# Four buffers for the down weights of a mixture of experts, and the last two items brought to their tokens by TensorE

## The chip, the core and the metric

The kernel runs on one core of a Trainium2 chip. The time is the device time of one execution in microseconds (us); less is better. The core has TensorE (PE, matmuls), VectorE (DVE), ScalarE (ACT), GpSimd (POOL) and SyncE (SP), each with an instruction stream of its own, and 16 DMA engines that all of them share. The engines meet at semaphores only.

## What is computed

A block of three layers on 512 tokens (8 sequences of 64) of width 512: cross attention, a linear attention, and a mixture of experts. The change is in the third alone:

```python
logits = xf @ gate_w.T                        # 512 tokens, 32 experts
top_w, top_i = lax.top_k(softmax(logits), 6)
h  = silu(einsum('ecd,edi->eci', xb, w1)) * einsum('ecd,edi->eci', xb, w3)   # xb: the tokens of each expert
ob = einsum('eci,eid->ecd', h, w2)            # w1, w3: 512 x 352, w2: 352 x 512 for each expert
y  = zeros((T, D)).at[t_s].add(ob[buf_idx] * w_s[:, None])
return x + y + silu(xf @ sw1) * (xf @ sw3) @ sw2
```

All of it is in float32.

## The kernel before

The first two layers take the first 690 us and are not touched. In the third, the shared experts are done as 8 items (`NSH`: two halves of the weights by four tiles of 128 tokens), while the router's result is turned into lists. Then come the **items** of the routed experts. An item is one expert with up to 128 of its tokens; an expert that has more than 128 gets a second item, next in the list. Here there are 36 items for 32 experts, so four items (1, 6, 13 and 26, counted from 0) are the second of their expert. How many there are, and which, is known only on the chip, so each engine runs a loop of two items a turn up to a value read from the list (`last_turn`), and reads what it needs for item m from rows of a small list in SBUF, `lst`, into a register: `item_value`, one read for one value. `ODD` of m is 1 if item m - 1 is a second item, `LOADED` is 1 if the item's weights are to be loaded, `HIGH` is half of m, `SLOT` says which of the two split copies of the up weights its expert has.

For item m the engines do this:

- **GpSimd** gathers 128 token rows three items ahead (`ex_gather`, indirect DMA) and scatters the result of item m - 2 with an addition into one of two arrays in HBM, `y_scratch` (`ex_scatter`, indirect DMA).
- **SyncE** issues the loads: `ex_load_w13` (two DMAs of 704 KB, for w1 and w3, into one of four raw slots of `w13_raw`), and `ex_load_w2` (512 KB and 192 KB, into one of **two** slots of `w2_raw`). A load whose expert is already there is issued with a condition that is 0, and moves nothing. In a turn the queue handles the up weights of item m + 3, then the down weights of item m. The latter wait until the down matmuls of item m - 2 are done (`d_ps`).
- **ScalarE** and **VectorE** split the raw up weights into a high and a low part (L888 and L892), as float32 is multiplied in three passes (`mm3`, L311 to L313).
- **TensorE** transposes the next item's tokens, does 24 up matmuls of item m (`ex_up`), the down matmuls of item m - 1 (`ex_down`, L876; these wait for the down weights, `w2_in`), and transposes h (`ex_hT`).

The queue's waits for down weights before:

```python
            if isinstance(m, int) and m == 0:
                e.wait_ge(d_ps, TT)
            else:
                e.wait_ge(d_ps, m + item_value(e, ODD, m) + (NSH - 1))
```

After the last item its result and the one before are scattered too. Then SyncE reads both `y_scratch` arrays back (L1176, L1179), VectorE adds them to x (L1661, L1665), and SyncE writes x out (L1182).

Of the kernel before, what the change touches and what calls it, by code (L numbers as in the profile page):

```python
# [31 lines left out]
P = 128  # L32
# [6 lines left out]
def perceiver_block(nc, x_in, ctx_in, ctxT_in, Wq, Wk, WkT, Wv, Wo, gq, gk,  # L39
# [17 lines left out]
    with stack:  # L57
# [144 lines left out]
        hot = sbuf(moe, "hot", [P, TT, TOP_K, E])  # L202
        hotp = sbuf(moe, "hotp", [P, TT, TOP_K, E])
# [7 lines left out]
        seats_and_items = sbuf(moe, "seats_and_items", [P, TT * TOP_K * (P + 2 * ML)])  # L211
        seat = seats_and_items[:, 0:TT * TOP_K * P].rearrange("p (q n) -> p q n", n=P)
        item = seats_and_items[:, TT * TOP_K * P:].rearrange("p (q a n) -> p q a n", a=2, n=ML)
        y_back = seats_and_items[:, 0:2 * TT * D].rearrange("p (k t d) -> p k t d", k=2, t=TT)
# [16 lines left out]
        EXPERT, LOADED, SLOT, ODD, HIGH = range(5)  # L231
        lst_f = sbuf(moe, "lst_f", [1, 5, ML + 1])
        lst_j = sbuf(moe, "lst_j", [1, ML + 1])
        lst = sbuf(moe, "lst", [1, 5, ML + 1], I32)
# [3 lines left out]
        w2_raw = sbuf(moe, "w2_raw", [P, 2, FC, D])  # L238
# [57 lines left out]
        y0_in, y1_in = sem("y0_in"), [sem(f"y1_in{t}") for t in range(TT)]  # L296
        y_sum, out_ready = sem("y_sum"), sem("out_ready")
# [581 lines left out]
        def raw_slot(e, m, k):  # L879

            if isinstance(m, int):
                return m % 4
            return item_value(e, HIGH, m) * 2 + k
# [40 lines left out]
        def ex_pe(e, i, k, first=False):  # L924

            m = i * 2 + k
            e.wait_ge(xeT_ready, m + 1)
            ex_pe_xT(e, 1 - k, i + (k + 1))
            e.wait_ge(h_ready, m + (NSH - 1))
            ex_up(lambda c: xeT_h[:, k, c, :], lambda c: xeT_l[:, k, c, :], k, item_value(e, SLOT, m), m * 2 + 6)  # L930
            ex_down(e, 1 - k, m + (NSH - 1), 1 if first else item_value(e, SLOT, m - 1),
                    (w2_in[1], 32) if first else (w2_in[1 - k], i * 32 + (k + 1) * 32), m + (NSH - 2))
            ex_hT(e, k, m + NSH)

        def ex_act(e, i, k):

            m = i * 2 + k
            odd = item_value(e, ODD, m + 1)
            ex_act_hT(e, 1 - k, m + (NSH - 1))
# [5 lines left out]
            raw = raw_slot(e, m + 1, 1 - k)  # L945
# [3 lines left out]
        def ex_dve_ob(e, i, k):  # L949

            m = i * 2 + k
            if not isinstance(i, int) or i > 1:
                e.wait_ge(acc_done[k], i * 16 - 16)
            e.tensor_copy(give[:, k:k + 1], tl[:, bass.ds(m - 2, 1)]).then_inc(give_ready, 1)
            e.wait_ge(d_ps, m + (NSH - 1))
            e.tensor_scalar(ob[:, k, :], ps[:, 6 + k, :], wl[:, bass.ds(m - 2, 1)], None, ALU.mult).then_inc(d_read, 1)  # L956
# [8 lines left out]
        def ex_dve(e, i, k):  # L965

            m = i * 2 + k
            ex_dve_xT(e, m + 1, 1 - k)
            ex_dve_take(e, m + 3, 1 - k)
            if isinstance(i, int) and i == 0:  # L970
                ex_dve_x(e, NSH - 2 + k)
            else:
                ex_dve_ob(e, i, k)
            ex_dve_h(e, k, m + NSH)
            if not isinstance(m, int) or m > 0:
                raw = raw_slot(e, m + 1, 1 - k)
# [15 lines left out]
        def ex_pool_scatter(e, m, k):  # L992

            e.wait_ge(give_ready, m - 1)
            e.wait_ge(d_read, m + (NSH - 1))
            e.sem_inc(acc_turn, 1)
            ex_scatter(e, k)

        def ex_pool(e, i, k):
# [6 lines left out]
            if not isinstance(i, int) or i > 0:  # L1006
                ex_pool_scatter(e, m, k)
# [4 lines left out]
        def load_w2(e, k, whole_ap, rest_ap, **cond):  # L1012
            e.dma_start(w2_raw[:, k, 0:FC - 1, :], whole_ap, **cond).then_inc(w2_in[k], 16)  # L1013
            e.dma_start(w2_raw[0:FW[-1], k, FC - 1, :], rest_ap, **cond).then_inc(w2_in[k], 16)  # L1014
# [8 lines left out]
        def ex_load_w13(e, m, k, before):  # L1023

            ex, new, raw = item_value(e, EXPERT, m, E - 1), item_value(e, LOADED, m), raw_slot(e, m, k)
            for n, w in enumerate((w1_r, w3_r)):
                if not isinstance(m, int) or m >= 2:
                    e.wait_ge(w13_ready, m * 2 + (n - 3))
                e.wait_ge(w13_in[k][n], before * 16)
                cond = {} if isinstance(m, int) and m < 2 else {"cond": new}  # L1030
                load_w13(e, k, n, raw, w[bass.ds(ex, 1)].rearrange("e p c f -> p (e c) f"), **cond)

        def ex_load_w2(e, m, k):
            ex, new = item_value(e, EXPERT, m, E - 1), item_value(e, LOADED, m)
            if isinstance(m, int) and m == 0:
                e.wait_ge(d_ps, TT)
            else:
                e.wait_ge(d_ps, m + item_value(e, ODD, m) + (NSH - 1))
            load_w2(e, k, w2_r[bass.ds(ex, 1)].rearrange("e p c d -> p (e c) d"),
                    w2_t[bass.ds(ex, 1)].rearrange("e p d -> p (e d)"), cond=new)  # L1040

        def last_turn(e):

            e.wait_ge(small_dve, DV_LISTS)
            return e.value_load(lst[0:1, EXPERT, ML:ML + 1], min_val=T * TOP_K // P // 2 - 1, max_val=MI // 2 - 1)

# [8 lines left out]
        def _(e):  # L1055
# [96 lines left out]
            def shared_rest():  # L1152
                for k in range(2):
                    load_w2(e, k, w2_r[E + k], w2_t[E + k])
# [9 lines left out]
            ex_load_w2(e, 0, 0)  # L1164
# [11 lines left out]
            e.dma_start(y_back[:, 0, :, :], y_dram[0].ap()[0:T, :].rearrange("(t p) d -> p t d", p=P)).then_inc(y0_in, 16)  # L1176
            e.wait_ge(acc_done[1], last_i * 16 + 16)
            for t in range(TT):
                e.dma_start(y_back[:, 1, t, :], y_dram[1].ap()[t * P:(t + 1) * P, :]).then_inc(y1_in[t], 16)  # L1179
# [3 lines left out]
            for k in range(2):  # L1183
                for s, n, uses in ((w13_in[k][0], 16, 5 - k), (w13_in[k][1], 16, 5 - k), (w2_in[k], 32, 3)):
                    e.wait_ge(s, last_i * n + uses * n)
                    e.sem_inc(past_loads, 1)
            e.wait_ge(past_loads, 6)
# [3 lines left out]
        def _(e):  # L1191
# [50 lines left out]
            e.tensor_tensor(gw_l[:, :, :], gw_raw[:, :, :], gw_h[:, :, :], ALU.subtract).then_inc(small_lo, 1)  # L1242
            last_i = last_turn(e)
# [9 lines left out]
            with e.Fori(2, last_i + 1) as i:  # L1253
                ex_pool(e, i, 0)
                ex_pool(e, i, 1)
            for k in range(2):
                ex_pool_scatter(e, last_i * 2 + (k + 2), k)

        @block.scalar
        def _(e):  # L1260
# [115 lines left out]
            ex_act_w13(e, 1, 0, 2, 1)  # L1376
            ex_act_w13(e, 1, 1, 2, 1)
# [3 lines left out]
            with e.Fori(1, last_act + 1) as i:  # L1381
                ex_act(e, i, 0)
                ex_act(e, i, 1)
            ex_act_hT(e, 1, last_act * 2 + (NSH + 1))

        @block.vector
        def _(e):
# [191 lines left out]
            def lists():  # L1579
# [9 lines left out]
                step(e.tensor_copy(lst_f[0:1, HIGH, 0:ML], iota_e[0:1, 0:ML]))  # L1589
                step(e.tensor_copy(lst[0:1, :, :], lst_f[0:1, :, :]))  # L1590
                step(e.tensor_scalar(lst[0:1, HIGH, 0:ML], lst[0:1, HIGH, 0:ML], 1, None, ALU.arith_shift_right))
                step(e.tensor_scalar(lst[0:1, EXPERT, ML:ML + 1], lst[0:1, EXPERT, ML:ML + 1], 1, None, ALU.arith_shift_right))
                e.tensor_scalar(lst[0:1, SLOT:HIGH + 1, :], lst[0:1, SLOT:HIGH + 1, :], 1, None, ALU.bitwise_and).then_inc(small_dve, 1)
# [54 lines left out]
            ex_dve_w13(e, 1, 0, 7, 1)  # L1648
            ex_dve_xT(e, 0, 0)
            ex_dve_take(e, 2, 0)  # L1650
            ex_dve_w13(e, 1, 1, 8, 1)
            for m in range(4):
                ex_dve(e, m // 2, m % 2)
            with e.Fori(2, last_i + 1) as i:
                ex_dve(e, i, 0)
                ex_dve(e, i, 1)
# [201 lines left out]
```

## Time and profile before

| | |
|---|---|
| median of 3 runs | 1063.48 us (1063.03 to 1066.78) |
| profiled execution: its own time | 1069.81 us |
| its span | 1068.0 us |
| granted TensorE clock, mean | 0.982 |
| PE busy in the span | 986.1 us (92%) |
| DVE, ACT, POOL busy | 62%, 51%, 25% |

The profile shows one execution. Its span begins with the first instruction; times in the rows are microseconds from there. Its own time is 6.3 us above the median of the runs without a profile, so differences are to be taken between profiled executions, or between medians. An engine's busy time doesn't count instructions that only handle registers, semaphores or the issue of DMAs; SyncE has no other kind, so the table has no row for it. `SPq` in a view is SyncE's stream.

### The profile page before, as it was taken

What the parts mean: (1) busy time and instruction counts of PE and PEld (TensorE: products, weight loads), DVE (VectorE), ACT (ScalarE), POOL (GpSimd) and SP (SyncE); (2) the same over time, 40 slices, a digit from 0 to 9 for tenths busy, and PEclk for the clock granted to TensorE, in tenths of its full rate; (3) what the DMA queues carried; (4) which work ended last, traced back from release to release, by engine and by line L of the source; (5) the groups of instructions that cost most, each with busy time, mean ns of one, the idle gap of its engine ahead of it and who ended that gap; (6) DMA issues with size and microseconds to landing.
All of it is one profiled execution on the core that took longest, in us unless ns stands there. A gap on an engine that the chain in (4) does not pass through costs nothing.

```text
span 1068.0 us, 18826 instructions
## 1 busy us (share of the span) xinstructions
PE 986.1 (92%) x5428; PEld 824.3 (77%) x5429; DVE 666.2 (62%) x994; ACT 543.1 (51%) x888; POOL 272.0 (25%) x188
## 2 busy tenths in 40 slices
PE   6999899999999869999999998799998999998792
PEld 5788699898998748888888886588776776776681
DVE  5645665667656557777777875557466666666563
ACT  5444666665666545555555525332454554554451
POOL 2200122121221133333222414200132232232222
PEclk9899999999999999999999999899999999999997
DMA  9000452332125041222112024106489999999986
GB/s 314 31 0 1 107 183 81 98 98 76 45 76 130 1 148 60 79 66 70 59 60 98 20 104 159 59 1 255 147 255 276 297 276 352 336 292 279 316 238 184
DMA packets 76059, 152.92 MB, mean 143 GB/s; under 512 B 11264, under 2 KB 38272, under 8 KB 75776
## 3 DMA queue, kind: packets, MB, share of 16 engines
q1 hardware_dynamic: 67728, 132.92, 37.1%
q0 software_dynamic: 8304, 19.67, 8.6%
q8 instruction: 14, 0.23, 0.1%
q14 instruction: 13, 0.11, 0.0%
HBM read 153.87 MB, written 14.55 MB: 158 GB/s over the span
## 4 chain that ended last, share of the span: by engine, by line
PE 63%; issue 12%; SPq 11%; DVE 4%; DMA 4%; ACT 3%; POOL 2%; ACTq 0%; DVEq 0%; POOLq 0%
PE ps L311 15%; PE ps L312 15%; PE ps L313 15%; SPq L847 6%; PE ps L672 6%; PE ps L876 4%; DMA w_raw<-in_w 2%; SPq L1010 2%; POOL wo_l L451 1%; SPq L1013 1%; SPq L1014 1%; PE ps L731 1%; PE ps L738 1%; PE ps L748 1%; PE ps L659 1%
## 5 line engine op out<-in xcount | busy, mean ns | idle before, releaser
L876 PE MATMUL ps<-w_raw,hT 128*128 (+3 forms) x264 | 124.3, 607 | 20.2 <-DMA w_raw<-in_w 17.8
L892 DVE TENSOR_TENSOR w_l<-w_raw,w_h 128x1408 fp32r<-128x1408 f32 x78 | 124.8, 1639 | 21.9 <-issue 13.2
L888 ACT ACTIVATE w_h<-w_raw 128x1408 fp32r (+1 forms) x78 | 103.3, 1369 | 25.1 <-issue 16.0
L694 POOL TENSOR_TENSOR lw_l<-lw_raw,lw_h 128x1024 fp32r<-128x1024 f32 x32 | 77.0, 2409 | 146.6 <-ACT lw_h L690 146.1
L985 POOL DMA_INDIRECT xe<-xn_scratch,take x39 | 39.2, 1004 | 259.1 <-DVE ob L956 173.2
L876 PEld LDWEIGHTS ps<-w_raw,hT 128*128 128x128 f32 (+1 forms) x264 | 48.0, 191 | 68.0 <-issue 67.7
L311 PE MATMUL ps<-w_h,xeT_h 128*128 x288 | 96.6, 335 | 1.6 <-DVE w_l L892 1.6
L313 PE MATMUL ps<-w_h,xeT_l 128*128 x288 | 93.4, 324 | 0.0
L312 PE MATMUL ps<-w_l,xeT_h 128*128 x288 | 92.9, 323 | 0.0
L311 PE MATMUL ps<-xT_hi,lw_h 128*128 128x512 f32 x192 | 77.3, 402 | 0.0
L312 PE MATMUL ps<-xT_lo,lw_h 128*128 128x512 f32 x192 | 76.5, 398 | 0.0
L901 DVE TENSOR_TENSOR h<-h,ps 128x352 f32<-128x352 f32 x44 | 22.9, 521 | 85.7 <-PE ps L313 59.8
L313 PE MATMUL ps<-xT_hi,lw_l 128*128 128x512 f32 x192 | 75.4, 393 | 0.0
L1395 DVE TENSOR_REDUCE ssk<-sqk 128x4 f32<-128x512 f32 (+1 forms) x64 | 43.6, 685 | 39.4 <-ACT sqk L1275 39.2
L906 ACT ACTIVATE hT<-ps 128x256 f32<-128x256 f32 x44 | 16.8, 383 | 99.5 <-PE ps L865 99.3
L1275 ACT ACTIVATE sqk<-ps 128x512 f32<-128x512 f32 x64 | 38.1, 598 | 49.8 <-PE ps L313 43.9
L311 PE MATMUL ps<-wk_h,cT_h 128*128 128x512 f32 (+1 forms) x128 | 52.2, 408 | 11.3 <-DVE cT_l L1391 8.7
L554 POOL TENSOR_TENSOR wq_l<-wq_raw,wq_h 128x1024 fp32r<-128x1024 f32 x8 | 19.3, 2411 | 170.0 <-ACT wq_h L514 170.0
L672 PE MATMUL ps<-pT,ctx 128*128 128x128 f32 x512 | 61.9, 277 | 0.4
L989 POOL DMA_INDIRECT y_scratch<-ob,give x36 | 57.2, 1588 | 15.8 <-issue 10.4
L672 PEld LDWEIGHTS ps<-pT,ctx 128*128 128x128 f32 x512 | 59.0, 192 | 2.0 <-ACT pT L544 2.0
L785 DVE RECIPROCAL q_r<-q_r 128x512 f32<-128x512 f32 x16 | 53.6, 3348 | 6.0 <-ACT q_r L761 6.0
(297 smaller groups left out, 2610.4 us busy)
## 6 DMA issues: line engine op xcount, KB each, us to landing
w_raw<-in_w SPq DMA_DIRECT2D x86, 704.0 KB
w_raw<-in_w SPq DMA_DIRECT2D x40, 512.0 KB
w_raw<-in_w SPq DMA_DIRECT2D x40, 192.0 KB
rkB<-rk_scratch SPq DMA_DIRECT2D x56, 128.0 KB, 3.2
wq_raw<-in_Wq SPq DMA_DIRECT2D x8, 512.0 KB, 4.7
wo_raw<-in_Wo SPq DMA_DIRECT2D x16, 256.0 KB, 2.9
lw_raw<-in_kwT SPq DMA_DIRECT2D x8, 512.0 KB, 3.4
lw_raw<-in_qwT SPq DMA_DIRECT2D x8, 512.0 KB, 3.3
```

The lines of the kernel that those rows point to most:

```text
L311: nc.tensor.matmul(out_ap, lh, rh, start=first, stop=False)
L312: nc.tensor.matmul(out_ap, lh, rl, start=False, stop=False)
L313: return nc.tensor.matmul(out_ap, ll, rh, start=False, stop=last)
L672: m = e.matmul(ps[:, 4 + j % 2, at:at + P], ctx[:, b * KPB + t, hcol(c)], pT[:, b, t, :], start=t == 0, stop=t == KPB - 1)
L694: e.tensor_tensor(lw_l[n][:, :, :], lw_raw[n][:, :, :], lw_h[n][:, :, :], ALU.subtract).then_inc(lw_ready[n], 1)
L785: e.reciprocal(q_r[:, k, :], q_r[:, k, :]).then_inc(q_recip, 1)
L847: return e.value_load(lst[0:1, row, bass.ds(m, 1)], min_val=0, max_val=most)
L876: m = e.matmul(ps[:, 6 + k, :], hT[r, k, c, :], w2_raw[r, slot(w), c, :], start=c == 0, stop=c == FC - 1)
L888: e.activation(w13_h[:, k, n, :, :], w13_raw[:, slot(raw), n, :, :], ACT.Copy).then_inc(w13_hi_s, 1)
L892: e.tensor_tensor(w13_l[:, k, n, :, :], w13_raw[:, slot(raw), n, :, :], w13_h[:, k, n, :, :], ALU.subtract).then_inc(w13_ready, 1)
L989: e.indirect_dma_start(y_dram[k].ap(), bass.IndirectOffsetOnAxis(ap=give[:, k:k + 1], axis=0), ob[:, k, :], None, compute_op=ALU.add).then ...
L1395: e.tensor_reduce(ssk[:, t, bass.ds(g * 4, 4)], sqk[:, t % 2, :].rearrange("p (h n) -> p h n", n=P), AX.X, ALU.add).then_inc(sqk_free, 1)
```

## The change

It does five things.

1. **Four down-weight slots.** `w2_raw` has four slots. They lie partly over the seats and items lists, which are dead once the tokens are listed, and the loads of items 2 and 3 wait for that (`small_ps`). An item's down weights are asked for four items ahead in SyncE's order and wait for the down matmuls of item m - 4.
2. **The expert's first slot.** `HIGH` gives way to `FIRST`, the raw slot of the expert's first item (0 to 3); a second item takes up and down weights from there. A slot is then in use an item longer, so a new row `HELD` says by how many items the wait is later. `LOADED` now holds for item 1 as well.
3. **The last turn is peeled** from the loops of all engines: no token transposes, gathers and splits for items behind the last. SyncE's loop ends two turns earlier, and GpSimd's and VectorE's one, with the turn ahead read from the list.
4. **The last two items go to tokens by TensorE**: VectorE makes `home` (128 seats by 512 tokens, 1 where the seat's token is the column), and TensorE multiplies it with the items' results into four banks of PSUM, which VectorE adds to x. They are not scattered.
5. **Order at the end**: SyncE waits for all loads before it reads y back, since y now lies over other tiles.

```diff
         def ex_load_w13(e, m, k, before):
 
-            ex, new, raw = item_value(e, EXPERT, m, E - 1), item_value(e, LOADED, m), raw_slot(e, m, k)
+            ex, new = item_value(e, EXPERT, m, E - 1), item_value(e, LOADED, m)
+            static = isinstance(m, int) and m < 4
+            raw, held = (m, 0) if static else (raw_slot(e, m), item_value(e, HELD, m, 3))
             for n, w in enumerate((w1_r, w3_r)):
-                if not isinstance(m, int) or m >= 2:
+                if not static:
+                    e.wait_ge(w13_ready, m * 2 + (held * 2 + (n - 3)))
+                    e.sem_inc(acc_turn, 1)
+                elif m >= 2:
                     e.wait_ge(w13_ready, m * 2 + (n - 3))
...
-        def ex_load_w2(e, m, k):
+        def ex_load_w2(e, m, k, before):
+
             ex, new = item_value(e, EXPERT, m, E - 1), item_value(e, LOADED, m)
-            if isinstance(m, int) and m == 0:
-                e.wait_ge(d_ps, TT)
+            w = m if isinstance(m, int) and m < 4 else raw_slot(e, m)
+            if isinstance(m, int) and m < 2:
+                e.wait_ge(d_ps, TT * (m + 1))
+            elif isinstance(m, int) and m < 4:
+                e.wait_ge(small_ps, PS_TOKENS)
             else:
-                e.wait_ge(d_ps, m + item_value(e, ODD, m) + (NSH - 1))
-            load_w2(e, k, w2_r[bass.ds(ex, 1)].rearrange("e p c d -> p (e c) d"),
+                e.wait_ge(d_ps, m + item_value(e, HELD, m, 3) + (NSH - 3))
+                e.sem_inc(acc_turn, 1)
+            e.wait_ge(w2_in[k], before * 32)
+            load_w2(e, k, w, w2_r[bass.ds(ex, 1)].rearrange("e p c d -> p (e c) d"),
                     w2_t[bass.ds(ex, 1)].rearrange("e p d -> p (e d)"), cond=new)
...
             for m in (2, 3, 4):
                 ex_load_w13(e, m, m % 2, m // 2 + 1)
-            ex_load_w2(e, 1, 1)
+            for m in (1, 2, 3):
+                ex_load_w2(e, m, m % 2, m // 2 + 1)
             for m in range(2):
                 ex_load_w13(e, m + 5, 1 - m, m + 3)
-                ex_load_w2(e, m + 2, m)
-            with e.Fori(1, last_i + 1) as i:
+                ex_load_w2(e, m + 4, m, 3)
+            with e.Fori(1, last_i - 1) as i:
                 for k in range(2):
                     ex_load_w13(e, i * 2 + (k + 5), 1 - k, i + (k + 3))
-                    ex_load_w2(e, i * 2 + (k + 2), k)
-            e.wait_ge(acc_done[0], last_i * 16 + 16)
...
+                    ex_load_w2(e, i * 2 + (k + 4), k, i + 3)
...
+            e.wait_ge(past_loads, 6)
+            e.wait_ge(acc_done[0], last_i * 16)
+            e.dma_start(y_back[0][:, :, :], y_dram[0].ap()[0:T, :].rearrange("(t p) d -> p t d", p=P)).then_inc(y0_in, 16)
...
+            for k in range(2):
+                e.tensor_scalar(home[:, k, :], iota_t[:, :], tl_f[:, 1, bass.ds(last_i * 2 + k, 1)], None,
+                                ALU.is_equal).then_inc(home_ready, 1)
...
+            e.wait_ge(home_ready, 2)
+            e.wait_ge(d_read, last_i * 2 + (NSH + 1))
+            to_tokens(0, 0)
+            ex_down(e, 1, last_i * 2 + (NSH + 1), item_value(e, FIRST, last_i * 2 + 1, 3), (w2_in[1], last_i * 32 + 64),
                     last_i * 2 + NSH)
+            for t in range(1, TT):
+                to_tokens(0, t)
+            e.wait_ge(d_read, last_i * 2 + (NSH + 2))
+            for t in range(TT):
+                to_tokens(1, t).then_inc(last_ps, 1)
```

What the built program has on **SyncE** in its loop, for the down weights of one item, before (`TENSOR_LOAD lst` reads one value of the list, `ISA` and `REGISTER_ALU` are instructions on registers):

```order
L847 ISA
L847 TENSOR_LOAD lst
L847 ISA x3
L847 TENSOR_LOAD lst
L847 ISA x3
L847 TENSOR_LOAD lst
L847 ISA x2
L1038 ISA
L1013 ISA [waits d_ps]
L1013 DMA w_raw<-in_w 128x1024
L1014 ISA
L1014 DMA w_raw<-in_w 96x512
```

The same place in the changed program, up to the wait for the DMA two items earlier:

```order
L852 ISA
L852 TENSOR_LOAD lst
L852 ISA x3
L852 TENSOR_LOAD lst
L852 ISA x3
L852 TENSOR_LOAD lst
L852 ISA x3
L852 TENSOR_LOAD lst
L852 ISA x2
L1058 ISA
L1060 REGISTER_ALU [waits d_ps]
L1025 ISA [waits w2_in0]
```

and on from there:

```order
L1025 REGISTER_ALU
L1025 DMA w_and_lists<-in_w 128x1024
L1026 ISA
L1026 REGISTER_ALU
L1026 DMA w_and_lists<-in_w 96x512
```

There are four reads for three, and three short instructions more. The up weights have a read more as well. Over the loop's two items the changed stream has 16 reads, 60 `ISA` and 7 `REGISTER_ALU`; the one before has 12, 52 and 2.

At the end of **TensorE**'s stream, before (the down matmuls of the last item):

```order
L870 REGISTER_ALU
L872 REGISTER_ALU [waits hT_ready]
L873 ISA [waits d_read]
L876 ISA [waits w2_in1]
L876 MATMUL ps<-w_raw,hT 128x512
L876 ISA
L876 MATMUL ps<-w_raw,hT 128x512
L876 ISA
L876 MATMUL ps<-w_raw,hT 128x512
L57 UNCONDITIONAL_BRANCH
```

and in the changed program:

```order
L1862 MATMUL ps<-ob,hots 128x512 [waits d_read,home_ready]
L852 ISA
L852 TENSOR_LOAD lst
L852 ISA x2
L881 ISA [waits w2_in1,d_read,hT_ready]
L881 MATMUL ps<-w_and_lists,hT 128x512
L881 ISA
L881 MATMUL ps<-w_and_lists,hT 128x512
L881 ISA
L881 MATMUL ps<-w_and_lists,hT 128x512
L1862 MATMUL ps<-ob,hots 128x512 x3
L1862 MATMUL ps<-ob,hots 128x512 [waits d_read]
```

One token matmul stands ahead of the last down matmuls, three behind them, and four more (the last row and three like it) wait for the last item's scaled result.

## Rows read from the trace of the kernel before

**Rows 1.** The page, part 2: busy tenths in 40 slices, the DMA engines.

```profile
DMA  9000452332125041222112024106489999999986
```

**Rows 2.** The waits, 760 to 1068: us in total, times, longest.

```profile
PE ps L876 <- DMA w_raw<-in_w: 17.8, 12, 2.4
```

**Rows 3.** The waits of SyncE's queue, 760 to 1060.

```profile
SPq L1013 <- PE ps L876: 38.9, 5, 16.2
```

**Rows 4.** TensorE's timeline, first up matmuls of three items: start, duration.

```profile
756.10 0.42 PE L311 MATMUL ps<-w_h,xeT_h 128*128 x1
...
1031.40 0.40 PE L311 MATMUL ps<-w_h,xeT_h 128*128 x1
...
1038.68 0.40 PE L311 MATMUL ps<-w_h,xeT_h 128*128 x1
...
1042.48 0.33 PE L313 MATMUL ps<-w_h,xeT_l 128*128 x1
```

**Rows 5.** SyncE's timeline, 765 to 1048: issues of up (L1010) and down weights (L1013).

```profile
777.82 0.34 SPq L1013 DMA_DIRECT2D w_raw<-in_w  x1
...
786.72 1.05 SPq L1010 DMA_DIRECT2D w_raw<-in_w  x2
...
875.06 0.35 SPq L1013 DMA_DIRECT2D w_raw<-in_w  x1
...
937.69 0.01 SPq L1013 DMA_DIRECT2D w_raw<-in_w  x1
944.42 0.01 SPq L1013 DMA_DIRECT2D w_raw<-in_w  x1
...
961.08 0.32 SPq L1013 DMA_DIRECT2D w_raw<-in_w  x1
...
979.38 0.34 SPq L1013 DMA_DIRECT2D w_raw<-in_w  x1
...
1018.40 0.35 SPq L1013 DMA_DIRECT2D w_raw<-in_w  x1
...
1047.87 0.08 SPq L1013 DMA_DIRECT2D w_raw<-in_w  x1
```

**Rows 6.** The chain that ended last, 1049 to 1050.4, along SyncE.

```profile
1049.01 0.05 SPq L847
...
1049.65 0.05 SPq L847
...
1049.75 0.27 SPq L847
...
1050.30 0.05 SPq L1028
```

**Rows 7.** GpSimd's timeline, a scatter; then the chain along SyncE.

```profile
1027.86 1.59 POOL L989 DMA_INDIRECT y_scratch<-ob,give  x1 [0.30 <-issue]
...
1027.88 0.71 issue
```

**Rows 8.** The chain: down weights on their way; a cast and a split.

```profile
778.44 5.19 DMA w_raw<-in_w
...
961.68 7.14 DMA w_raw<-in_w
...
864.70 1.39 ACT w_h L888
...
866.24 1.64 DVE w_l L892
```

**Rows 9.** The end: timeline and chain, 1044 to 1068.

```profile
1046.64 2.84 PE L876 MATMUL ps<-w_raw,hT 128*128 x6 [0.91 <-ACT hT L907]
...
1054.58 5.74 DMA seats_and_items<-y_scratch
...
1060.35 2.50 DVE L1661 TENSOR_TENSOR x<-x,seats_and_items 128x512 f32<-128x512 f32 x4 [9.99 <-DMA seats_and_items<-y_scratch]
1062.76 2.49 DVE L1665 TENSOR_TENSOR x<-x,seats_and_items 128x512 f32<-128x512 f32 x4
```

More of the change, by code:

```diff
@@ L228, in perceiver_block @@
         m_hot = sbuf(moe, "m_hot", [P, ML])
-        EXPERT, LOADED, SLOT, ODD, HIGH = range(5)
-        lst_f = sbuf(moe, "lst_f", [1, 5, ML + 1])
+        EXPERT, LOADED, SLOT, ODD, FIRST, HELD = range(6)
+        lst_f = sbuf(moe, "lst_f", [1, 6, ML + 1])
         lst_j = sbuf(moe, "lst_j", [1, ML + 1])
-        lst = sbuf(moe, "lst", [1, 5, ML + 1], I32)
+        lst = sbuf(moe, "lst", [1, 6, ML + 1], I32)
         w13_raw = sbuf(moe, "w13_raw", [P, 4, 2, DC, FF])
@@ L877, in ex_down, with raw_slot @@
             m.then_inc(d_ps, 1)
[L879 to L883, printed above, removed]
+        def raw_slot(e, m):
+            return item_value(e, FIRST, m, 3)
         def ex_act_w13(e, k, n, use, raw):
@@ L922, in ex_pe_xT, with ex_pe, ex_act @@
             last.then_inc(xeT_ps, 1)
-        def ex_pe(e, i, k, first=False):
+        def ex_pe(e, i, k, first=False, last=False):
             m = i * 2 + k
             e.wait_ge(xeT_ready, m + 1)
-            ex_pe_xT(e, 1 - k, i + (k + 1))
+            if not last:
+                ex_pe_xT(e, 1 - k, i + (k + 1))
             e.wait_ge(h_ready, m + (NSH - 1))
             ex_up(lambda c: xeT_h[:, k, c, :], lambda c: xeT_l[:, k, c, :], k, item_value(e, SLOT, m), m * 2 + 6)
-            ex_down(e, 1 - k, m + (NSH - 1), 1 if first else item_value(e, SLOT, m - 1),
+            ex_down(e, 1 - k, m + (NSH - 1), 1 if first else item_value(e, FIRST, m - 1, 3),
                     (w2_in[1], 32) if first else (w2_in[1 - k], i * 32 + (k + 1) * 32), m + (NSH - 2))
             ex_hT(e, k, m + NSH)
-        def ex_act(e, i, k):
+        def ex_act(e, i, k, last=False):
             m = i * 2 + k
+            ex_act_hT(e, 1 - k, m + (NSH - 1))
+            if last:
+                ex_act_silu(e, k, m + NSH)
+                return
             odd = item_value(e, ODD, m + 1)
-            ex_act_hT(e, 1 - k, m + (NSH - 1))
+            raw = None if isinstance(m, int) and m == 0 else raw_slot(e, m + 1)
             ex_act_xT(e, m + 1, 1 - k)
@@ L1380, in _ @@
             ex_act(e, 0, 1)
-            with e.Fori(1, last_act + 1) as i:
+            with e.Fori(1, last_act) as i:
                 ex_act(e, i, 0)
                 ex_act(e, i, 1)
+            ex_act(e, last_act, 0)
+            ex_act(e, last_act, 1, last=True)
             ex_act_hT(e, 1, last_act * 2 + (NSH + 1))
@@ L1808, in _, with to_tokens @@
             ex_pe(e, 0, 1)
-            with e.Fori(1, last_i + 1) as i:
+            with e.Fori(1, last_i) as i:
                 ex_pe(e, i, 0)
                 ex_pe(e, i, 1)
-            ex_down(e, 1, last_i * 2 + (NSH + 1), item_value(e, SLOT, last_i * 2 + 1), (w2_in[1], last_i * 32 + 64),
-                    last_i * 2 + NSH)
+            ex_pe(e, last_i, 0)
+            ex_pe(e, last_i, 1, last=True)
+            def to_tokens(k, t):
+                return e.matmul(ps[:, t, :], home[:, k, t * P:(t + 1) * P], ob[:, k, :], start=k == 0, stop=k == 1)
+            e.wait_ge(home_ready, 2)
+            e.wait_ge(d_read, last_i * 2 + (NSH + 1))
+            to_tokens(0, 0)
+            ex_down(e, 1, last_i * 2 + (NSH + 1), item_value(e, FIRST, last_i * 2 + 1, 3), (w2_in[1], last_i * 32 + 64),
+                    last_i * 2 + NSH)
+            for t in range(1, TT):
+                to_tokens(0, t)
+            e.wait_ge(d_read, last_i * 2 + (NSH + 2))
+            for t in range(TT):
+                to_tokens(1, t).then_inc(last_ps, 1)
 def kernel(x, ctx_1024, L0_xattn_Wq, L0_xattn_Wk, L0_xattn_Wv, L0_xattn_Wo, L0_xattn_gq, L0_xattn_gk,
```

127 lines of the change are left out of this document (74 added, 53 removed).

## The prediction

> **What bounds it now.** I read, in this order: the page's slices, the waits, TensorE's timeline, SyncE's own timeline, the chain, and the end. Only the last 310 us matter: the edit touches nothing before the expert items. In those the DMA engines are 80 to 90% busy [rows 1], and the waits name one thing on TensorE: 12 down matmuls (L876) wait for their weights, 17.8 us in all [rows 2]. TensorE starts the first item's up matmuls at 756.10 and the 36th's at 1038.68; two neighbours undisturbed are 7.28 us apart (1031.40 to 1038.68) [rows 4]. 35 x 7.28 = 254.8 against 282.6 measured: 27.8 us are lost, 17.8 of them to those waits.
>
> Why do the weights come late? It looks as if a buffer were missing: the load of item m's down weights waits for item m - 2's down matmuls. But SyncE's queue waits for TensorE only 5 times, 38.9 us, the longest 16.2 [rows 3]. Everywhere else SyncE is just working: its down-weight issues (L1013) come 7.8 us apart where every load is carried out: 875.06 to 937.69 is 8 steps, 944.42 to 961.08 is 2, 979.38 to 1018.40 is 5: 118.3 us for 15 steps, **7.89 us a step** [rows 5], more than TensorE's 7.28. The stage is paced by the instruction stream of the queue that issues the loads, not by the number of buffers.
>
> What a step consists of is seen in the chain, which near its end runs along SyncE. A value read from the list into a register (`item_value`, L847) is three or four instructions: the address 0.05, the read 0.27, two more behind it. From one address to the next, 1049.01 to 1049.65, is 0.64 us; from a read to what follows its group, 1049.75 to 1050.30, is 0.55 [rows 6]. Six such reads are some 3.7 us of the 7.89. Once per item, while GpSimd issues a scatter (L989, 1.59 us from 1027.86), SyncE stands almost still: from 1027.88 on 0.71 us pass without an instruction [rows 7].
>
> **The change, part by part.**
>
> *Reads on SyncE.* A loop step had 3 reads for the up weights and 3 for the down weights; now it has 4 and 4 (FIRST in place of HIGH, HELD added; FIRST and HELD in place of ODD). The built order for two items has 16 reads for 12, 60 register instructions for 52, and 7 short ones for 2. So per item: two reads with their two followers, 2 x 0.55 = 1.10, and 2.5 short instructions at some 0.07 (the address takes 0.05 and its read starts 0.10 after it; this is under that) = 0.17: **+1.27 us**. 7.89 + 1.27 = **9.16 us a step**. Nothing hides it: the stream has no waits to fall into. The freeze is one scatter per item as before. Bounds: the reads' own duration alone, 2 x 0.27 = 0.5 a step; or 2 x 0.64 + 2.5 x 0.1 + a tenth more freeze, 1.6.
>
> What a page says: the Trainium skill ("Runtime: NRT & Kernel Launch", Instruction fetch mechanics) puts a register load at about 200 ns. The read's own 0.26 here is near that, but the whole group takes 0.55 to 0.64; by the page's figure the step would grow by 0.6, to 8.5, which is the second rival below.
>
> *Where SyncE starts.* Its last long wait is unchanged: item 2's down weights waited until 777.82 for item 1's down matmuls; now item 4's do, for the same event (item 1 is a second item of its expert, so HELD is 1). From there to item 7's up weights there were 8 reads, 786.72 [rows 5]; now 12 and some short ones: +2.7, **789.4**. Items 2 and 3 go out before, at about 765; that gives TensorE two loads of lead, which the slow stream eats: it loses 1.88 us an item on TensorE.
>
> *To the last loads.* From item 7's to item 35's up weights are 28 steps: 28 x 9.16 = 256.5. Of them 2 up-weight pairs and 3 down-weight pairs aren't carried out (the experts with two items); an issue that isn't is 0.08 instead of 0.35 [rows 5]; ten issues, -2.7. Item 35's up weights: 789.4 + 256.5 - 2.7 = **1043.2**. Its down weights follow one step and the down half of the reads later (9.16 + 4.2, less 0.5 for the unissued pair of item 36): **1056.1**.
>
> *TensorE's end.* From an up-weight issue: second half 0.7 later, landing 6.2 after that (between 5.2 and 7.1), cast 1.39, split 1.64, gaps 0.3 [rows 8], half of the up matmuls 2.0 (all take 4.1, 1038.68 to 1042.81, [rows 4]): 12.2, so up is done at 1055.4; before, at 1042.8. The last down matmuls ended at 1049.48 [rows 9]; now 12.6 later, and 0.6 more for the one token matmul put ahead of them: 1062.7. In the steady part TensorE stands for about 1.9 us an item waiting for split up weights; the down matmuls wait for nothing.
>
> *The tail.* Before: 18.5 us from the last down matmul (1049.48) to the end (1068.0): SyncE's leftover steps, then the way back of y from 1054.58, 5.74 us [rows 9], 8 additions (1060.35 to 1065.25), 2.8 us for the last output. The scatters were under that. The token matmuls: 8 of 128x128 by 512 columns in f32, like the 3 of a down group that take 2.84: 0.9 each; 5 of them behind the last down weights' matmuls or in the shade of its scaling, done by 1069. y can't start before SyncE has counted all loads (that wait now stands ahead of y, since the buffers overlap): item 35's down weights, 1056.1 + 0.6 for the second part, landing 4.2 (light traffic; 5.2 to 7.1 under load), 0.3: 1061.2. Then 5.7 for y0, 12 additions of 0.625 = 7.5 (four more than before, all on VectorE), 2.8 for the output: 1061.2 + 5.7 + 7.5 + 2.8 = **1077.2**. By TensorE alone it would be 1062.7 + 0.9 + 7.5 + 2.8 = 1073.9, the gain of 7.3 which the tail would have given.
>
> *The rest.* The two comparisons for `home` (128x512 on VectorE, under 1 us each) replace the splits of item 36, the iota on GpSimd falls in its wait for the lists, four more steps on the lists are 0.2 each before SyncE starts, well ahead of 777. ACT's read moves ahead of its wait; in a stage that waits for SyncE it gives nothing. Uncovered they would cost about 2 us together.
>
> **Sum.** 1077.2 - 1068.0 = +9 us in the profiled execution (its own time 1069.8). Its 6.3 us over the median of 1063.5 is a constant around the program, I take it, not time in the stream: 1063.5 + 9 = **1072.5**. [...]
>
> **The rivals.**
> - *SyncE paces, and the added reads cost their duration only* (0.5 to 0.6 a step; for it: the read is 0.26, and some would run while the queue is frozen anyway; against: SyncE is held during the freeze, so it catches nothing up). The step is 8.43, 29 steps x 0.73 less: 1077.2 - 21.2 = 1056.0, which is 12 faster: **1051.5**. This is the case on the other side. It decides from a step of 8.85: (1077.2 - 1068.0) / 29 = 0.31 under 9.16.
> - *The buffers were the cause after all* (for it: the wait list; against: 15 steps without one wait of SyncE): the 17.8 go, and the tail's 7.3: **1038.5**.
> - *The transfers were the bound* (for it: DMA near 9 tenths [rows 1]; the same bytes are moved, less two scatters; against: a down load lands in 5.2 to 7.1 us, hardly a queue): only the tail and two loads of lead would come back, while the reads cost nothing: **1056**.
> - *Slower still:* a standing TensorE may be granted half its clock, and the freeze may grow with the longer step: 9.5 a step, 29 x 0.34 = +10: **1082**.
>
> **How the numbers follow.** My forecast (step 9.0 to 9.3, +4.5 to +13) 0.55; costlier step 0.12; step between 8.7 and 9.0 (1060 to 1068) 0.15; the three faster ones together 0.18. A measurement here tells 0.5%, 5.3 us, from no change. Slower by more: 0.12, 0.50 of the first and a little of the next, 0.66; within: 0.17; faster: 0.17. The range leaves out the buffers' case and the far end of the costliest, and holds the cheap reads only in part: 1053 to 1081. The likeliest case's own is 1067 to 1077.
>
> **What would show it.** SyncE's down-weight issues 9.1 to 9.2 us apart with 8 reads between, and no waits on TensorE after the first 30 us; no down matmul waiting for its weights, but up matmuls waiting for the split, the split for the cast, the cast for the transfer, and TensorE's items 9.2 apart at the end; DMA share down from 9 to 7 or 8 tenths; y's issue near 1061 instead of 1054.6 and 12 additions after it. I am wrong if the steps are under 8.85, or if SyncE waits for TensorE in the later half: then the reads were paid for by waits that this trace doesn't show.

## The result, and the profile after

The change makes the kernel slower.

| | before | after |
|---|---|---|
| median of the runs beside each other | 1065.13 us (1063.03 to 1067.63) | 1081.11 us (1079.56 to 1082.91) |
| ratio, 95% interval | 1 | 1.015 [1.0116, 1.0184] |
| the profiled execution: own time, span | 1069.81, 1068.0 | 1082.91, 1081.1 |

Measured twice more, on chips 6 and 0, each time beside the kernel before, the ratio was 1.0231 [1.0167, 1.0296] and 1.0134 [1.0106, 1.0162]. The forecast was 1072.5 us with a range up to 1081: right in sign, far short in size.

The waits of the changed kernel from 760 to 1082, those that touch the experts' weights (us in total, times, longest):

```profile
ACT w_h L891 <- DMA w_raw<-in_w: 78.0, 45, 4.4
DVE w_l L895 <- ACT w_h L891: 57.5, 29, 3.6
...
PE ps L316 <- DVE w_l L895: 32.4, 21, 2.6
```

The wait of [rows 2] has no counterpart: no down matmul (now L881) waits for its weights. In its place stands a chain of three waits on the *up* weights: the cast for the transfer, the split for the cast, TensorE for the split. A transfer that comes late can be late because it is long or because it was asked for late, and SyncE's own waits tell which, as [rows 3] did:

```profile
SPq L1025 <- PE ps L881: 4.0, 1, 4.0
SPq L1059 <- PE ps L881: 3.5, 1, 3.5
SPq L1205 <- DMA w_and_lists<-in_w: 2.2, 1, 2.2
```

Until all loads are out, SyncE now waits twice, 7.5 us in all, where it waited 38.9 before. All the rest of the stage it executes instructions (the third row is behind the last load). Its timeline, at some issues of up weights (now L1022), answers to [rows 5]:

```profile
791.32 1.08 SPq L1022 DMA_DIRECT2D w_raw<-in_w  x2
...
881.48 1.09 SPq L1022 DMA_DIRECT2D w_raw<-in_w  x2
...
955.41 1.10 SPq L1022 DMA_DIRECT2D w_raw<-in_w  x2
...
1047.27 1.09 SPq L1022 DMA_DIRECT2D w_raw<-in_w  x2
```

From 881.48 to 955.41 are 8 steps: 9.24 us each, against 7.89 before and 9.16 forecast. The first row is item 7's load (forecast 789.4), the last is item 35's (forecast 1043.2).

TensorE on the last item, in the timeline; in brackets stands how long it was idle and for what:

```profile
1055.09 0.42 PE L316 MATMUL ps<-w_h,xeT_h 128*128 x1 [2.41 <-DVE w_l L895]
...
1055.69 0.49 PE L316 MATMUL ps<-w_h,xeT_h 128*128 x1
1055.98 0.49 PE L317 MATMUL ps<-w_l,xeT_h 128*128 x1
...
1059.62 0.32 PE L316 MATMUL ps<-w_h,xeT_h 128*128 x1
1059.78 0.32 PE L317 MATMUL ps<-w_l,xeT_h 128*128 x1
...
1060.42 0.32 PE L318 MATMUL ps<-w_h,xeT_l 128*128 x1
```

It had stood for 2.41 us. The first three matmuls start 0.26 to 0.16 us apart, the next eleven 0.29, and the rest 0.16. The windows of these stretches (length; busy us and instructions of PE, PEld, DVE, ACT, POOL; granted clock; DMA share; GB/s) say why:

```profile
1052.70:1055.10 2.40, 0.01 (x1) 0.02 (x1) 1.62 (x1) 0.85 (x2) 0.00 (x0) 1.00 1.02 266
1055.70:1058.90 3.20, 3.20 (x12) 3.20 (x12) 2.65 (x5) 1.18 (x4) 0.00 (x0) 0.50 0.18 59
1059.10:1060.50 1.40, 1.40 (x11) 1.40 (x10) 0.29 (x1) 0.00 (x0) 0.33 (x1) 1.00 0.00 0
1000.00:1040.00 40.00, 34.32 (x165) 27.71 (x166) 23.19 (x33) 17.90 (x28) 10.30 (x8) 0.96 0.95 290
```

The granted clock was still 1.00 (2.4 GHz) in the idle stretch, 0.50 (1.2 GHz) from 1055.70 to 1058.90, and 1.00 again from 1059.10 on. From 1000 to 1040 its mean is 0.96.

The end, timeline. It answers to [rows 9]; L1862 are the matmuls that bring the last two items to the tokens, L1208 and L1210 ask for the two halves of y, and L1703, L1707 and L1711 are the 12 additions:

```profile
1059.59 0.36 SPq L1025 DMA_DIRECT2D w_and_lists<-in_w  x1
...
1063.83 0.39 SPq L1208 DMA_DIRECT2D xn_c<-y_scratch  x1
...
1065.44 2.84 PE L881 MATMUL ps<-w_and_lists,hT 128*128 x6
1065.52 0.39 SPq L1210 DMA_DIRECT2D w_and_lists<-y_scratch  x1
1068.12 6.17 PE L1862 MATMUL ps<-ob,hots 128*128 128x512 f32 x14
...
1070.93 2.50 DVE L1703 TENSOR_TENSOR x<-x,xn_c 128x512 f32<-128x512 f32 x4 [1.69 <-DMA xn_c<-y_scratch]
1073.52 2.50 DVE L1707 TENSOR_TENSOR x<-x,w_and_lists 128x512 f32<-128x512 f32 x4
1075.93 2.47 DVE L1711 TENSOR_TENSOR x<-x,ps 128x512 f32<-128x512 f32 x4
```

The last down matmuls end at 1068.28, 18.8 us later than before. From there to the end it is 12.8 us; before it was 18.5. So the tail gives 5.7 back, and TensorE's late end takes over three times that: +13.1 in the span.

### The profile page after: what moved, and what is told of

Read it like the earlier page. It is cut to its first block, busy times and chain, and to the rows that moved or that the text cites. A ratio compares the mean times of both kernels' runs of the same rounds, so it can differ in the third digit from the quotient of the medians.

```text
span 1081.1 us, 19087 instructions
## 1 busy us (share of the span) xinstructions
PE 998.6 (92%) x5440; PEld 834.6 (77%) x5441; DVE 667.9 (62%) x998; ACT 539.4 (50%) x885; POOL 268.8 (25%) x185
## 2 busy tenths in 40 slices
DMA packets 75278, 150.46 MB, mean 139 GB/s; under 512 B 11120, under 2 KB 38128, under 8 KB 74992
## 4 chain that ended last, share of the span: by engine, by line
PE 55%; SPq 17%; issue 13%; DVE 6%; DMA 4%; ACT 3%; POOL 2%; DVEq 0%; POOLq 0%; ACTq 0%
PE ps L316 14%; PE ps L317 14%; PE ps L318 14%; SPq L852 10%; PE ps L677 6%; SPq L1022 2%; DMA w_raw<-in_w 2%; PE ps L881 2%; SPq L1025 1%; SPq L1026 1%; POOL wo_l L456 1%; PE ps L736 1%; PE ps L743 1%; PE ps L753 1%; PE ps L349 1%
## 5 line engine op out<-in xcount | busy, mean ns | idle before, releaser
L316 PE MATMUL ps<-w_h,xeT_h 128*128 x288 | 99.9, 347 | 32.6 <-DVE w_l L895 32.4
L881 PE MATMUL ps<-w_and_lists,hT 128*128 (+3 forms) x264 | 121.0, 594 | 0.0
L317 PE MATMUL ps<-w_l,xeT_h 128*128 x288 | 96.5, 335 | 0.0
L318 PE MATMUL ps<-w_h,xeT_l 128*128 x288 | 96.2, 334 | 0.0
L316 PEld LDWEIGHTS ps<-w_h,xeT_h 128*128 128x128 f32 x288 | 57.0, 198 | 37.5 <-issue 37.5
L881 PEld LDWEIGHTS ps<-w_and_lists,hT 128*128 128x128 f32 (+1 forms) x264 | 48.3, 189 | 43.3 <-issue 42.9
```

The source lines that it names most:

```text
L316: nc.tensor.matmul(out_ap, lh, rh, start=first, stop=False)
L317: nc.tensor.matmul(out_ap, lh, rl, start=False, stop=False)
L318: return nc.tensor.matmul(out_ap, ll, rh, start=False, stop=last)
L881: m = e.matmul(ps[:, 6 + k, :], hT[r, k, c, :], w2_raw[r, slot(w), c, :], start=c == 0, stop=c == FC - 1)
```

## The experiments

**Theory.** SyncE's instruction stream sets the time from about item 8 on, at one step for each item, and the two added reads in a step, with the few instructions that come with them, cost some 1.3 us together. **First rival:** the reads are cheap; the extra buffers, the new order or the tail cost the time. **Second rival:** the transfers are the bound, and SyncE only looks busy.

### Take away one read of each half step

HELD (by how many items the wait for a slot is later) is taken as the constant 1 on SyncE; everything else of the change stays. The step has 6 reads again. For most items this also asks for one item's work more to be done before a slot is free, as HELD is 1 only for the item three behind a second one.

```diff
-            raw, held = (m, 0) if static else (raw_slot(e, m), item_value(e, HELD, m, 3))
+            raw, held = (m, 0) if static else (raw_slot(e, m), 1)
...
-                e.wait_ge(d_ps, m + item_value(e, HELD, m, 3) + (NSH - 3))
+                e.wait_ge(d_ps, m + 1 + (NSH - 3))
```

> The changed kernel, with HELD not read but taken as 1 for every item: SyncE has 6 reads a step, as before the change, instead of 8; slots, peeling and token matmuls stay. Theory (the reads pace SyncE, and SyncE paces the items): steps of 9.2 us become 8.0, the time falls by 28 x 1.2 = 34 us at most, less where TensorE's own 7.28 us takes over; 1045 to 1055 us. Rival (the four slots, the longer waits or the token matmuls cost the time): it stays at 1078 to 1083.

Measured: 1048.73 us (1047.72 to 1048.99), the kernel before beside it 1068.93: ratio 0.9792 [0.9739, 0.9845]. Two reads a step are the whole of the loss and more: without them the change *gains* some 20 us. Eight steps of SyncE (the same items as 881.48 to 955.41 above) take 64.3 us, 8.04 each, where the changed kernel had 9.24:

```profile
869.33 0.96 SPq L1022 DMA_DIRECT2D w_raw<-in_w  x2
...
933.67 0.96 SPq L1022 DMA_DIRECT2D w_raw<-in_w  x2
```

Its wait list shows the same chain of waits, shorter:

```profile
ACT w_h L891 <- DMA w_raw<-in_w: 36.5, 29, 3.0
DVE w_l L895 <- ACT w_h L891: 18.5, 17, 2.5
...
PE ps L316 <- DVE w_l L895: 6.7, 12, 1.5
```

### Add two unused reads to each loop step, before and after

```diff
+            if not isinstance(m, int):
+                item_value(e, ODD, m)
...
+            if not isinstance(m, int):
+                item_value(e, SLOT, m)
```

The first stands ahead of the up weights, the second ahead of the down weights. (After: SLOT in both places.) First the kernel before, where 6 reads become 8:

> The kernel before, with two more list reads in each step of SyncE's loop (one ahead of the up weights, one ahead of the down weights), whose values nobody uses. Theory: steps of 7.9 us become 9.1 to 9.2; from the seventh item on 28 steps or more are each 1.2 us longer: plus 25 to 35 us, 1090 to 1100. Rival (the reads are hidden in the freezes, or SyncE isn't what paces): within 5 us of before.

Measured: 1114.04 us (1110.58 to 1116.87), ratio 1.0398 [1.0336, 1.046]: 45.1 us more, beyond the 25 to 35 that were expected. The eight steps that took 62.6 us in [rows 5] take 75.7 here, 9.46 each:

```profile
885.11 0.35 SPq L1013 DMA_DIRECT2D w_raw<-in_w  x1
...
960.83 0.35 SPq L1013 DMA_DIRECT2D w_raw<-in_w  x1
```

That is 1.57 us a step over the 7.89 of before, not the 1.2 to 1.3 of the expectation. (The 45.1 us over the 34 steps of the loop are 1.33, but not every step of before was on the path.) Then the changed kernel, 8 reads to 10:

> The changed kernel with two more unused reads a step of SyncE, 10 instead of 8. Theory: every microsecond of the stream is on the path, 28 to 29 steps x 1.2 = plus 34 us, 1115. Rival (something else paces the changed kernel): under 5 us.

Measured: 1126.31 us (1125.13 to 1127.11), 45.2 over the median of the changed kernel, which was measured in another session; over 30 loop steps that is 1.5 us. By its trace the step is 10.47 us, 1.23 over 9.24:

```profile
900.09 1.09 SPq L1022 DMA_DIRECT2D w_raw<-in_w  x2
...
983.88 1.09 SPq L1022 DMA_DIRECT2D w_raw<-in_w  x2
```

Two reads that do nothing cost either kernel about as much a step as the change's two, and no byte was added.

### Take the reads away for good

Item m's up and down loads are issued in one step and its four values are read once for both: 4 reads a step. The down weights then go out one item later than in the change. Of the edit, the loop:

```diff
...
-                    ex_load_w13(e, i * 2 + (k + 5), 1 - k, i + (k + 3))
-                    ex_load_w2(e, i * 2 + (k + 4), k, i + 3)
+                    values = item_values(e, i * 2 + (k + 3))
+                    ex_load_w13(e, i * 2 + (k + 3), 1 - k, i + (k + 2), values)
+                    ex_load_w2(e, i * 2 + (k + 3), 1 - k, i + (k + 2), values)
...
```

> The changed kernel, with SyncE handling the up and the down weights of the same item in a step, so that the four values are read once: 4 reads a step instead of 8. Nothing else differs. Theory: the step is 9.2 - 4 x 0.62 = 6.7 us, under TensorE's 7.28, so TensorE paces: the items take about 36 x 7.3, and the tail is shorter: 1035 to 1045. Rival (the DMA engines can't go faster than in the kernel before): 1055 to 1065.

Measured: 1045.33 us (1044.61 to 1049.76), ratio 0.9773 [0.9716, 0.983]. It beats both kernels. The second rival falls here: the pages of the two kernels give the same 150.46 MB moved, and this one is 36 us faster. Four steps in which SyncE waits for nothing take 26.7 us, 6.67 each, as the theory had it:

```profile
886.07 1.13 SPq L1022 DMA_DIRECT2D w_raw<-in_w  x2
...
912.73 1.13 SPq L1022 DMA_DIRECT2D w_raw<-in_w  x2
```

So the step follows the number of reads in it, whatever else differs:

| reads in a step | kernel | us a step |
|---|---|---|
| 4 | shared reads | 6.67 |
| 6 | before, two profiles | 7.89, 7.61 |
| 6 | HELD constant | 8.04 |
| 8 | before with two reads more | 9.46 |
| 8 | changed, three profiles | 9.24, 9.48, 9.17 |
| 10 | changed with two reads more | 10.47 |

The second and third profiles are shown below. Fetching a longer loop is not what costs: the pages count 27 packets on the instruction queues in the whole execution before and 30 after. SyncE's waits with shared reads:

```profile
SPq L1063 <- PE ps L881: 21.6, 4, 7.0
...
SPq L1025 <- DMA w_and_lists<-in_w: 5.8, 6, 1.5
```

Now SyncE waits for buffers again, repeatedly, so the stream is no longer the bound. What is next was not tested: the cast waits 49.1 us for transfers, 36 times, and TensorE's items come 7.24 apart where nothing is late.

### What asking earlier is worth

The kernel with HELD constant 1 and four slots, but with the order and the wait of before: item m's down weights behind item m + 1's up weights, released by item m - 2's down matmuls.

```diff
-                e.wait_ge(d_ps, m + 1 + (NSH - 3))
+                e.wait_ge(d_ps, m + (NSH - 1))
...
-                    ex_load_w2(e, i * 2 + (k + 4), k, i + 3)
+                    ex_load_w2(e, i * 2 + (k + 2), k, i + 2)
```

> The changed kernel with HELD as the constant 1 (six reads a step) and with the order and the ask of before: item m's down weights go behind item m + 1's up weights and wait for the down matmuls of item m - 2, though four slots are there. It tells whether the four buffers or the earlier ask were worth anything once the reads cost no more than before. If asking early is what takes away the 17.8 us that 12 down matmuls of before waited: those waits come back, 12 to 20 us in all, and the time is 12 to 18 us over that of the kernel with HELD 1 and the early ask: 1061 to 1067. If SyncE's instruction stream alone sets the time, both have six reads a step and end alike within 4 us: 1045 to 1053, with waits on the up weights' cast instead.

Measured: 1066.91 us (1064.29 to 1072.15) beside 1066.66 of before: ratio 0.9999 [0.9977, 1.0021]. The wait of [rows 2] is back:

```profile
PE ps L881 <- DMA w_and_lists<-in_w: 20.9, 12, 2.9
```

Twelve waits and 20.9 us; before had 12 and 17.8. So the early ask is worth 18.2 us by the two medians (1066.91 - 1048.73), or 22 by the two ratios, as the kernels ran on different chips, as long as the step is short. One thing is not separated. Here SyncE waited 16.9 us in 14 places for the slots of the up weights, which the kernel before never did, so some of the 18 may come from the constant HELD, with which SyncE waits an item longer for most slots (in the kernel with the early ask that wait was 1.4 us, twice). For the same reason the ratio of 0.9999 says only that the peeled turn, the tokens by TensorE and this wait come to nothing together, not that each does.

### The scatter's part in the step

[Rows 7] show SyncE standing still while GpSimd issues a scatter. In both kernels the scatters were left out: a count on the semaphore stands in for the indirect DMA, so that y lacks most routed items.

```diff
-            e.indirect_dma_start(y_dram[k].ap(), ..., compute_op=ALU.add).then_inc(acc_done[k], 16)
+            e.sem_inc(acc_done[k], 16)
```

> The kernel before without the scatters of the expert items' results to y (the indirect DMA is left out, a count on its semaphore stands in its place, so y lacks the routed experts' part). It tells what the moments cost in which SyncE stands nearly still while GpSimd issues a scatter. If the scatter's issue is what holds SyncE: some 0.8 us a step less, the step of 7.89 falls to about 7.1, under TensorE's 7.28, and TensorE's items come 7.3 to 7.5 apart: 15 to 22 us faster, 1042 to 1050. If the long gaps of SyncE have another cause, they stay, 50 of over 0.6 us between 800 and 1040, the step stays at 7.7 to 7.9 and the time falls by 5 us at most.

Measured: 1053.11 us (1051.8 to 1054.22), ratio 0.9869 [0.9849, 0.9889], 3 us over the expected stretch. SyncE's timeline, two down-weight issues 8 steps apart:

```profile
870.82 0.35 SPq L1012 DMA_DIRECT2D w_raw<-in_w  x1
...
928.69 0.01 SPq L1012 DMA_DIRECT2D w_raw<-in_w  x1
```

7.23 us a step, 0.66 under 7.89, and 0.31 under the 7.54 that the same eight steps take in the second profile of before (below). Stretches of over 0.6 us in which SyncE starts nothing, between 800 and 1040, fall from 51 to 9. Then the changed kernel:

> The changed kernel without the scatters of the expert items' results (the indirect DMA is left out, a count on its semaphore stands in its place, so y lacks the part of most routed items). The same edit to the kernel before took 13.6 us off and brought its step from 7.7 to 7.9 down to 7.2. If the added reads are instructions of SyncE that nothing covers, the step without scatters is 7.2 + 1.3 to 1.5 = 8.5 to 8.7, still over TensorE's 7.28, and the time is (8.6 to 7.3) x 30 = some 40 us over the stage's floor: 1056 to 1066. If the scatters are as good as free in the changed kernel, as their first trace suggests (SyncE starts 8.9 instructions in the first 1.5 us of one), the step stays at 9.1 to 9.2 and the time within 4 us of the changed kernel's.

Measured: 1068.65 us (1066.89 to 1070.66), ratio to before 1.0022 [1.0, 1.0045]; the changed kernel with its scatters had 1079.82 on that chip. The time is 2.7 us above what the theory said. The up-weight issues, 8 steps apart:

```profile
887.00 1.08 SPq L1021 DMA_DIRECT2D w_raw<-in_w  x2
...
957.34 0.58 SPq L1021 DMA_DIRECT2D w_raw<-in_w  x2
```

8.79 us a step. With no scatter to disturb either, the change lengthens the step by 8.79 - 7.23 = **1.56 us**; with scatters it is 9.24 - 7.89 = 1.35. Each of these sets one session against another, and the step of one and the same kernel differs by 0.3 between sessions. On one chip, 0, the scatters cost the changed kernel's step 9.17 - 8.79 = 0.38. The claim that they had become as good as free is refuted: leaving them out took 11.2 us off.

### Both kernels profiled again

> The kernel before, profiled a second time. The prediction took 6.3 us off its profiled execution, as a constant that the profile adds. If that is so, the second profiled execution is again 5 to 7 us over the median of the runs beside it. If the first profile was only one of the longer executions of a kernel whose executions differ by several us, the second one's own time lies anywhere between 1063 and 1073, and the more likely value is the median, 1065 to 1069; the difference from the first is then to be found in the place of the last up matmuls (1038.68 there) and of item 35's loads.

Measured: own time 1065.86 with a span of 1064.1; the median of the eight runs of that kernel in the same session was 1071.33 (up to 1074.07), ratio 1.0006 [0.9976, 1.0036]. This profiled execution lies 5.5 us *below* its median. The first up matmul of the last item (at 1038.68 in [rows 4]) and the waits of [rows 2]:

```profile
1034.66 0.40 PE L311 MATMUL ps<-w_h,xeT_h 128*128 x1
```

```profile
PE ps L876 <- DMA w_raw<-in_w: 14.2, 10, 2.4
```

Four microseconds earlier, with ten waits for twelve: the difference between the profiles is one of the stage. The same stretch of 8 steps that took 62.6 us in [rows 5] (875.06 to 937.69) goes here from 874.89 to 935.18, 60.3, or 7.54 each; over the prediction's 15 steps it is 7.61 for 7.89.

```profile
874.89 0.35 SPq L1013 DMA_DIRECT2D w_raw<-in_w  x1
...
935.18 0.00 SPq L1013 DMA_DIRECT2D w_raw<-in_w  x1
```

> The changed kernel, profiled a second time, to see how well one profile gives its step. If the step of SyncE is set by the instructions alone, the issues of the up weights come 9.2 us apart again (8 steps from about 881 in 73 to 75 us), the last loads go out within 3 us of 1047.3 and 1059.6, and the own time is 1079 to 1084. If executions of this kernel differ as those of the kernel before do, by up to 10 us, the step is anywhere between 9.0 and 9.5.

Measured: 1093.52 us (2 runs) beside 1071.42, ratio 1.0231 [1.0167, 1.0296]. The own time, 1093.35, is 9 us above the 1079 to 1084 of the first case. Eight steps took 75.9 us, 9.48 each, which is within the 9.0 to 9.5 of the second: executions of this kernel differ too. Beside the 7.54 of before in the same session it is 1.94 more:

```profile
887.60 1.09 SPq L1022 DMA_DIRECT2D w_raw<-in_w  x2
...
963.46 0.34 SPq L1022 DMA_DIRECT2D w_raw<-in_w  x1
```

A third time, on another chip:

> The changed kernel once more, on whichever chip comes, with its second half against the kernel before. The two measurements so far gave 1081.1 against 1065.1 and 1093.5 against 1071.4, so the ratio 1.015 or 1.023. If the speed of SyncE's instructions beside the scatters differs from chip to chip, and this sets the size, the ratio lies between 1.014 and 1.026 and goes with the step: 9.2 us gives 1081, 9.6 gives 1093, some 0.4 us a step for 12 us. If it is chance within one chip, the runs of this kernel here spread over more than 8 us.

Measured: 1079.82 us (1078.56 to 1081.66) beside 1065.87, ratio 1.0134 [1.0106, 1.0162]; 9.17 us a step:

```profile
879.73 1.09 SPq L1022 DMA_DIRECT2D w_raw<-in_w  x2
...
953.11 1.09 SPq L1022 DMA_DIRECT2D w_raw<-in_w  x2
```

The ratio is just under the expected ratios. The four runs lie within 3.1 us of each other, and so did the four of the first measurement (3.4): the spread is between sessions. The second and the third ran on different chips, so these runs can't tell session from chip. The step goes with it: 9.17, 9.24, 9.48 for 1079.8, 1081.1, 1093.5. In SyncE's timeline the difference is partly beside the scatters: in the first 1.5 us of a scatter it started 9.0, 8.9 and 7.2 instructions. Why is not settled.

## Why the prediction was wrong in size

**The step that failed** is the last one of the sum: "Its 6.3 us over the median of 1063.5 is a constant around the program". It isn't. What lies around the program is the own time less the span: 1.7 to 2.0 us in all twelve profiles, and 1.7 to 2.1 in the runs without one. It is in the median as well, so it cancels, and all of the 6.3 us were time in the stream: that execution was one of the longer ones of a kernel whose runs lie between 1061.7 and 1077.8. Its longer waits of TensorE (17.8 us against 14.2 in the second profile) are not in the sum for the changed kernel, which follows SyncE's steps to the end, so there was nothing there to take them off from. The changed kernel's profiled own time is 1082.91 beside a median of 1081.11, that with HELD constant 1047.72 beside 1048.73, the shared reads' 1044.61 beside 1045.33, that of before at its second profile 1065.86 beside 1071.33. These pairs lie between +1.8 and -5.5 us. The Trainium skill ("Runtime: NRT & Kernel Launch", The ~15µs preamble/postamble breakdown) gives a gap of about 6.2 us, close to this 6.3, but between two other times: the profile's total and the execution time that the runtime reports. It says nothing of profiled against unprofiled executions, and no run here shows that gap. Set against the profiled execution alone, +9.2 would have given 1079.0, inside the range.

The miss of 8.6 us is 6.3 of this, plus 4.1 by which the spans differ more than forecast (13.1 for 9.0), less 1.8 by which the changed kernel's profiled execution lies over its median. The size of the change was missed as well: +9 forecast, 16.0 by the medians beside each other (1081.11 - 1065.13).

**The rest, by its steps.**

- *SyncE paces, and reads are what it is paced by:* right. Reads were added or taken away in four experiments, and step and time followed each time. For the kernel before it is half of the story: three of SyncE's five waits (2.7, 5.8 and 4.4 us) came behind an expert's second item, ahead of its issues at 817.07, 875.06 and 979.38, and down matmuls waited soon after, at 823.83, 880.95 and 984.85. So the wait for a slot had a part in the late weights too; how large a part was not separated.
- *+1.27 a step:* too small. The profiles give 1.35 (first pair), 1.94 (second pair, one session), 1.56 without scatters, 1.57 and 1.23 where two reads were added. That the step came out at 9.24 for 9.16 is in part luck: the 7.89 under it was high (7.61 in the second profile; in the first, four undisturbed steps of 7.5 us, 817.07 to 832.15 and 839.57 to 854.41, had been left out, with them it is 7.80), and the addition was low. The count of instructions was right; the price of the followers was not. SyncE starts 43 instructions a step in the kernel before without scatters (1377 in 240 us, 31.8 steps) and 53.5 in the changed one (1471, 27.5 steps): 10.5 more by this count, 8.5 by the built order, for 1.56 us is 0.15 to 0.18 each, gaps included. The 0.07 taken for the short ones was half of that. The end of the range, 1.6, held in all but the second pair. The Trainium skill ("Runtime: NRT & Kernel Launch", Instruction fetch mechanics) gives a register load about 200 ns; there it is a load from HBM, here a list in SBUF is read. An estimate by that figure is 0.6 a step, less than half of what was measured: the read's own row is near it (0.27), the group that it needs is not.
- *The start, 789.4:* it was 791.32. 1.35 of it is the release, which came at 779.17 instead of 777.82. "For the same event" held, but TensorE's event was itself later: its items began at 756.64 instead of 756.10, and the first took 7.83 instead of 7.33.
- *28 steps to item 35's up weights, 253.8 us:* 255.95, 2.1 more.
- *From that issue to the end of the up matmuls, 12.2 us:* 13.5. The forecast had half the clock only among its rivals; the rows above show it, 1.4 us for 11 matmuls. These three make the 5.3 us by which TensorE's up matmuls of the last item end late (1060.74 for 1055.4).
- *The tail:* y's issue came at 1063.83 for 1061.2, and y took 7.1 us for 5.7; 12 additions took 7.5 and the output 2.7, as forecast. 1063.83 + 7.10 + 7.47 + 2.70 = 1081.1, the span. That the return of y and not TensorE ends last was right.
- *What was to be seen:* no waits of the down matmuls, three waits in a row on the up weights, 12 additions: all there. The DMA share did not fall to 7 or 8 tenths: it was 0.95 from 1000 to 1040, at 290 GB/s. It reads nearly full while SyncE waits for no transfer, and the shared reads take 36 us off with the same bytes, so it was no measure of how near the transfers were to being the bound.
- *The rival of the buffers* (1038.5) was judged too harshly. Asking earlier is worth 18 us with a step of 8.04, just about the 17.8 of [rows 2]. The prediction treated "paced by the stream" and "helped by an earlier ask" as exclusive. They are not: at 8.04 us a step TensorE's 7.24 is nearly kept up with, and its items come in time up to item 19 (from item 20 on they are 7.9 apart); at 9.24 the same lead is used up by item 13, whose successor starts 10.0 us after it. The change bought some 18 us and paid some 32 for it (1081.11 - 1048.73, two sessions).

## What to carry to other kernels

Count what the queue that issues the loads executes for one item, reads and all, and take some 0.17 us for each instruction (7.23 us for 43, 8.79 for 53.5 here), or 0.6 to 0.8 us (0.95 in one pair of profiles) for each further value read from a list. Compare that with the pitch of the compute engine before adding a buffer whose bookkeeping needs another value; where two loads of one item need the same values, read them once. An earlier ask and a cheap stream act on the same waits: the ask was worth 18 us on a step of 8.04, a shorter step alone (the scatters left out) was worth 13.6, and what the ask is worth on the step of 9.24 was not measured. Measure each with the other held. And take a forecast's sum against the profiled execution's own time, or profile twice: the gap between a profile and the median is no constant when a kernel's executions differ by several microseconds.

## What was not expected of the hardware

- SyncE's speed is not the same from one session (and chip) to the next: the same program took 9.17, 9.24 and 9.48 us a step, and 1079.8 to 1093.5 us in all, while the kernel before varied from 1065.1 to 1071.4 in the medians.
- While GpSimd issues a scatter (1.6 us), SyncE started 4.8 instructions in the first 1.5 us in the first profile of before, 6.3 in its second, 5.1 with HELD constant, 8.9 in the changed kernel; elsewhere some 8 to 9. How much it is held back depends on something that these runs don't show; that leaving out the scatters shortens the step, by 0.3 to 0.66 us before and by 0.38 after on one chip, is shown in both kernels.
- Behind 2.4 us in which it stood idle, TensorE was granted half its clock from 1055.70 to 1058.90, in the last item of the changed kernel; a late item can so cost more than its wait.
